# One layer's experts, batch by batch, inside the next stage of a one-core kernel

## The chip, the cores and the metric

The kernel runs on one core of a Trainium2 chip. Its time is the device time of one execution in microseconds (us), as the median of several runs. The engines are TensorE (PE; its weight loads are shown as PEld), VectorE (DVE), ScalarE (ACT), GpSimd (POOL) and SyncE (SP, which issues the DMAs). Each runs its own instruction stream in order; they meet only at semaphores and at barriers between blocks and stages.

## What is computed

The input x has 2 batches of 512 tokens with 128 features. Four layers are added to it in turn:

```python
x = x + L0_xcond(layernorm(x), ...)   # stage A: self attention, cross attention, gated feed forward
x = x + L0_ffn(layernorm(x), ...)     # stage B: rms norm, causal attention, router, 31 experts and a shared one
x = x + L1_xcond(layernorm(x), ...)   # stage C: six layers of self attention, cross attention, feed forward
x = x + L1_ffn(layernorm(x), ...)     # stage D, run in the tail of stage C: a router and 64 experts
```

The part that the change is about is the end of the second and the beginning of the third:

```python
gates = jnp.sum(jax.nn.one_hot(topi, E_R) * topv[..., None], axis=-2)          # 3 of 31 experts
h = jax.nn.gelu(jnp.einsum('bsd,edh->besh', an, re_w1) + re_b1[None, :, None, :])
routed = jnp.einsum('bse,besh,ehd->bsd', gates, h, re_w2) + jnp.einsum('bse,ed->bsd', gates, re_b2)
return shared + routed + an + attn_out
```

Every expert is computed for every token and weighted with its gate, which is zero for most. The shared expert is the 32nd, with a gate of one.

## The kernel before

The 1024 tokens are T = 8 tiles of P = 128 tokens; B = 2 batches have TB = 4 tiles each. `m.x` is the residual stream, `m.y` the running sum of a layer, `m.xn` a normalised copy, and `m.hT` its transpose, [128 features, 2 batches, 512 tokens].

`build` (L141) runs stage A, B and C one after the other. `next_stage` (L154) clears and frees every semaphore taken since the last one and puts a barrier of all engines between stages; `m.sem` takes a semaphore and notes it for that. Two semaphores are taken ahead of stage A and used in both stages (L186): `m.later_loaded`, for the load of the affine weights of 18 later norms (`normw_later`, issued at L1067 in stage A), and `m.bias_loaded`. In stage B `norm_block` "B0n" normalises x twice (`norm_steps`: statistics of all tiles, a chain of small 128x8 operations for the reciprocal root, and one apply per tile); on PE it waits for later_loaded, runs `embed` (72 small matmuls at L222), and then transposes xn (L369). Meanwhile SP loads the attention weights (L1045) and the experts' weights in eight chunks (L1146). `self_attention_block`, another norm block and `router_b` follow.

`experts_b` (a block of its own) has 32 experts, and per expert e and batch b: an "up" matmul of 128x512 into bank b (L1246), a gelu on ACT (L1281), a "down" of four 128x128 matmuls (L1254), and four additions y = y + gate * down on DVE (L1300). PE's order is up(e, b), down(e-1, b), batches alternating. f32 matmuls appear as two records each.

Stage C begins behind a barrier. SP loads the first layer's weights (`w`), the rotary tables, the masks and `wx`, the weights of all layers' cross-attention keys and values. POOL sets constants (L2158 to L2163, L2192) and builds the selector `sel` with eight affine_selects (L2196). DVE computes the layer norm of x for all eight tiles (`norm_steps`), then unit 0's first norm (L2363 to L2375), then constants. A unit is one layer for one batch; there are 12. Their work is laid out by hand in tables of slots (TENSOR, VECTOR, SCALAR, GPSIMD, SYNC, by operation): unit n's operation in slot s stands at n * WINDOW + s with WINDOW = 1214, and each engine issues its list in the order of these numbers. A slot is no time: it gives only the order. Unit 0 begins with NORM1 at slot 364, its projections (L1844, L1851), the split of q and k into three bf16 parts by DVE, ACT and POOL, and their stacking by 12 DMAs (L2091); the first scores (L1765) stand at slot 581 and their row maxima (L2384) from 594 on. The second batch, unit 1, enters 1214 slots later, so nothing stands beside unit 0 until then. The K and V tables of cross attention (`tables`) are worked in between unit 0's first 26 scores.

`merged` sorts a second list of steps in with the units' own; so far only stage D's steps (`experts_plan`) use it. Banks of PSUM are handed out by `take` (a fixed bank) and `fill` (a ring of banks 5 to 7), with a "filled" and an "emptied" semaphore for each.

## Time and profile before

| | us |
|---|---|
| median of 3 runs | 2744.12 (2743.93 to 2749.65) |
| the profiled execution, its time | 2760.86 |
| its span, first to last instruction | 2759.1 |
| mean granted PE clock in it | 0.898 |

The profile page gives each engine's busy time over the span. A view by windows cuts the span and gives busy times, the granted clock (1.00 is 2.4 GHz, 0.50 is 1.2 GHz) and the DMA share in each window. The timeline lists instructions in order of time, with the idle time of the engine before them and what ended it.

### The profile page before, as it was taken

What the parts mean: (1) busy time and instruction counts of PE and PEld (TensorE: products, weight loads), DVE (VectorE), ACT (ScalarE), POOL (GpSimd) and SP (SyncE); (2) the same over time, 40 slices, a digit from 0 to 9 for tenths busy, and PEclk for the clock granted to TensorE, in tenths of its full rate; (3) what the DMA queues carried; (4) which work ended last, traced back from release to release, by engine and by line L of the source; (5) the groups of instructions that cost most, each with busy time, mean ns of one, the idle gap of its engine ahead of it and who ended that gap; (6) DMA issues with size and microseconds to landing.
All of it is one profiled execution on the core that took longest, in us unless ns stands there. A gap on an engine that the chain in (4) does not pass through costs nothing.

```text
span 2759.1 us, 32148 instructions
## 1 busy us (share of the span) xinstructions
PE 2273.3 (82%) x11288; PEld 900.5 (33%) x11288; DVE 1707.3 (62%) x3854; ACT 1132.3 (41%) x1855; POOL 143.3 (5%) x143
## 2 busy tenths in 40 slices
PE   5999969589999594698788788778878878877898
PEld 2333334343333373222222322223223232222433
DVE  4666748525666467676577567467657746755464
ACT  2333323102222131356366455646636645553421
POOL 0000000011110003000000000000000000010000
PEclk9999979769999697679799888979979988997999
DMA  3000000110000001000010001001001000020000
GB/s 137 1 1 1 1 0 1 65 43 1 1 1 1 1 1 65 26 24 1 23 40 1 24 1 40 1 24 40 2 23 40 1 24 1 24 96 0 1 0 8
DMA packets 38033, 54.33 MB, mean 20 GB/s; under 512 B 5074, under 2 KB 34547, under 8 KB 36339
## 3 DMA queue, kind: packets, MB, share of 16 engines
q1 hardware_dynamic: 37874, 52.28, 6.0%
q8 instruction: 93, 1.52, 0.2%
q14 instruction: 66, 0.53, 0.1%
HBM read 32.34 MB, written 0.52 MB: 12 GB/s over the span
## 4 chain that ended last, share of the span: by engine, by line
PE 38%; DVE 11%; ACT 8%; issue 4%; SPq 0%; ACTq 0%; DMA 0%; DVEq 0%
PE ps L1799 7%; PE ps L1784 5%; ACT C_prob L2226 4%; PE ps L1765 4%; DVE C_nm L2384 3%; PE ps L1844 3%; PE ps L1903 2%; PE ps L2012 2%; PE ps L1915 2%; ACT C_u L2304 2%; PE ps L2008 2%; PE ps L2033 2%; PE ps L1922 2%; PE ps L1880 2%; PE ps L1931 2%
## 5 line engine op out<-in xcount | busy, mean ns | idle before, releaser
L2384 DVE TENSOR_REDUCE C_nm<-ps 128x1 f32<-128x512 f32 x768 | 501.1, 684 | 207.7 <-PE ps L1765 202.7
L2226 ACT ACTIVATE C_prob<-ps 128x512 f32<-128x512 f32 x768 | 427.5, 596 | 248.6 <-PE ps L1784 238.8
L1765 PE MATMUL ps<-C_attn 62*128 62x512 bf16 x768 | 285.3, 428 | 65.9 <-DVE C_nm L2384 45.7
L1784 PE MATMUL ps<-C_attn 64*128 64x512 bf16 x768 | 259.6, 407 | 62.9 <-ACT C_prob L2226 52.0
L1799 PE MATMUL ps<-C_prob,C_attn 128*32 128x512 f32 x1536 | 223.4, 656 | 13.8 <-ACT C_prob L2226 13.8
L1765 PEld LDWEIGHTS ps<-C_attn 62*128 62x128 bf16 x768 | 64.6, 95 | 316.6 <-DVE C_nm L2384 153.1
L1784 PEld LDWEIGHTS ps<-C_attn 64*128 64x128 bf16 x768 | 59.5, 94 | 285.5 <-ACT C_prob L2226 204.5
L711 DVE TENSOR_REDUCE A_nm<-ps 128x2 f32<-128x1024 f32 x64 | 77.5, 1211 | 113.8 <-PE ps L494 113.7
L2304 ACT ACTIVATE C_u<-ps,C_biasx 77x512 f32<-77x512 f32 x192 | 115.5, 678 | 53.6 <-PE ps L1907 53.4
L2480 DVE TENSOR_REDUCE C_nmx<-ps 128x4 f32<-128x308 f32 x192 | 78.4, 470 | 60.7 <-PE ps L1884 60.5
L644 ACT ACTIVATE A_p<-ps 128x1024 f32<-128x1024 f32 x64 | 65.6, 1025 | 112.1 <-PE ps L522 112.1
L644 ACT ACTIVATE B_p<-ps 128x1024 f32<-128x1024 f32 (+1 forms) x64 | 45.0, 703 | 146.7 <-PE ps L526 146.7
L2639 DVE TENSOR_TENSOR C_prob<-C_prob,ps 128x512 f32<-128x512 f32 x64 | 43.9, 686 | 94.2 <-PE ps L2012 74.3
L2346 ACT ACTIVATE C_prob<-ps 128x512 f32<-128x512 f32 (+1 forms) x66 | 39.4, 597 | 151.9 <-PE ps L2008 149.6
L1844 PE MATMUL ps<-C_hT,C_w 128*128 128x512 f32 x144 | 89.1, 729 | 11.6 <-ACT C_hT L2250 6.2
L1300 DVE SCALAR_TENSOR_TENSOR y<-ps,B_gates,y 128x128 f32<-128x128 f32 x256 | 71.9, 344 | 42.0 <-PE ps L1254 42.0
L452 PE MATMUL ps<-hT,B_w 128*128 128x512 f32 x128 | 75.6, 674 | 23.4 <-DVE B_rot L706 12.2
L1880 PE MATMUL ps<-C_kc,C_qx 32*128 32x308 f32 x384 | 49.0, 584 | 41.9 <-DVE C_nmx L2480 20.0
L1838 PE MATMUL ps<-ident,xn 128*128 128x128 f32 x144 | 27.4, 321 | 67.4 <-DVE xn L2375 67.4
L494 PE MATMUL ps<-A_k,A_q 64*128 64x512 f32 x256 | 76.1, 672 | 4.9 <-DVE A_nm L711 4.9
L1254 PEld LDWEIGHTS ps<-B_w,B_h 128*128 128x128 f32 x512 | 68.1, 194 | 30.7 <-issue 30.7
L2406 DVE RECIPROCAL C_rden<-ps 128x16 f32<-128x16 f32 x96 | 24.3, 253 | 82.8 <-PE ps L1807 53.3
(376 smaller groups left out, 3855.1 us busy)
## 6 DMA issues: line engine op xcount, KB each, us to landing
C_attn<-C_first SPq DMA_DIRECT2D x144, 128.0 KB, 2.4
C_w<-in_C_w SPq DMA_DIRECT2D x6, 1090.0 KB, 5.1
C_attn<-in_D_ew SPq DMA_DIRECT2D x4, 1536.0 KB, 11.1
B_w<-in_B_ew SPq DMA_DIRECT2D x8, 514.0 KB, 10.8
normw_later<-in_norm_w SPq DMA_DIRECT2D x1, 2304.0 KB
A_w<-in_A_w SPq DMA_DIRECT2D x2, 1024.0 KB, 11.5
A_w<-in_A_w SPq DMA_DIRECT2D x2, 768.0 KB, 7.9
B_w<-in_B_w SPq DMA_DIRECT2D x1, 1536.0 KB, 9.7
```

Source lines behind the costliest of these rows:

```text
L494: last = pe.matmul(ps[:, S_BANK + h, 0:keys(t)], lhsT=qT[half(h), n % 3, t * P:(t + 1) * P], rhs=kT[half(h), n % 3, 0:keys(t)], start=True ...
L644: act.activation(prob[:, n % 2, kt, :, q0:S], ps[:, ST_BANK:ST_BANK + 2, q0:S], ACT.Exp, scale=SCALE)\
L711: dve.tensor_reduce(nm[:, n % 2, t, :], ps[:, S_BANK:S_BANK + 2, 0:keys(t)], AX.X, ALU.max, negate=True).then_inc(max_done, 1)
L1765: pe.matmul(ps[:, bank, :], lhsT=qs[side(hp, MAX_ROW), b, 2 * q + pq, t * P:(t + 1) * P], rhs=ks[side(hp, MAX_ROW), b, 2 * q + pq, :], sta ...
L1784: pe.matmul(ps[:, bank, :], lhsT=ks[side(1 - hp, HALF), b, 2 * q + pq, kt * P:(kt + 1) * P], rhs=qs[side(1 - hp, HALF), b, 2 * q + pq, :], ...
L1799: last = pe.matmul(ps[ct * VW:(ct + 1) * VW, PV_BANK, :], lhsT=va[:, b, kt, q * QUAD + ct, :], rhs=prob[:, kt % 2, ct // 2, ct % 2, :], st ...
L1844: pe.matmul(ps[:, bank, :], lhsT=weight(n, col), rhs=hT[:], start=True, stop=True)\
L1880: pe.matmul(ps[:, banks[r], 0:4 * CTX], lhsT=qx[rows, t * P:(t + 1) * P], rhs=cross.k[rows, c, :, :], start=True, stop=False)
L2226: act.activation(prob[:, kt % 2, pq, 1 - hp, :], ps[:, bank, :], ACT.Exp, scale=SCALE)\
L2304: act.activation(probx[:, q % 2, r, :], ps[0:CTX, bank, :], ACT.Exp, bias=cross.bias[:, b:b + 1], scale=SCALE).then_inc(emptied[bank], 1)
L2384: dve.tensor_reduce(nm[:, q % 2, t, pq, hp:hp + 1], ps[:, bank, :], AX.X, ALU.max, negate=True).then_inc(emptied[bank], 1)
L2480: dve.tensor_reduce(nmx[:, t, 4 * r:4 * r + 4], ps[:, bank, 0:4 * CTX].rearrange("p (j k) -> p j k", k=CTX), AX.X, ALU.max, negate=True).t ...
```

## The change

The experts of stage B leave their own block and become steps of stage C's order.

- `experts_b` is gone. The new list `first_plan` puts its work at negative and early slots: `bias_b`, then 65 steps `expert` on PE, ACT and DVE, first the 32 of batch 0 (20 slots apart, from slot -475 to 165) and then the 32 of batch 1 (18 slots apart, to 741 on PE). Step k on PE is up(k) followed by down(k-1). `up_bank` alternates banks 0 and 1 for batch 0 and is bank 2 alone for batch 1; `down_bank` alternates 3 and 4. The hidden tile h has two buffers, in place of four.
- The layer norm of x at the start of stage C is made batch by batch (`first_norm`, three parts each): batch 0 at slots 196 to 232, batch 1 at 772 to 852. DVE's constants come in ten parts among batch 0's experts.
- The cross-attention tables are steps of the plan too (`tables_v` from slot 861, `tables_k` from slot 921). `wx` is loaded only after the last expert, since its place in memory now holds the experts' weights.
- Memory is shared: the experts' weights with `prob` and `shared`, h and the transposed gates with `cw` and `cwx`, the gates and b2 with `cn`. Waits are added where the sharing asks for them (the first EXP, the first COPY_SUMS, the first WEIGH).
- The load semaphores change: later_loaded is taken inside stage A, counts both late loads, and SP waits for it at stage A's end. The waits for it and for bias_loaded in stage B are gone. The experts' chunks share one semaphore, for which SP waits in `router_b`.

```diff
-            m.later_loaded, m.bias_loaded = m.sem("later_loaded"), m.sem("B1_bias_loaded")
...
             if later is not None:
-                normw, w_loaded = later
-                pe.wait_ge(w_loaded, 16)
-                embed(pe, m, normw, 18, emb_done)
+                embed(pe, m, later, 18, emb_done)
...
-            if rope is not None:
-                act.wait_ge(bias_loaded, 16)
...
+    later_loaded = m.sem("later_loaded")
...
+        @block.sync
+        def _(sp):
+            sp.wait_ge(later_loaded, 32)
+
...
+            sp.wait_ge(experts_loaded, 16 * (E_MOE // B_CHUNK + 1))
...
+B_STRIDE = 20
+B_STRIDE_1 = 18
+FIRST_NORM = 110
+B_LAST = VECTOR[0]["STATS1"][0] - FIRST_NORM
+B_FIRST = B_LAST - 30 - E_MOE * B_STRIDE
+B_END = B_LAST + E_MOE * B_STRIDE_1
+WX_LOAD = 90
+WX_STRIDE = 30
+CONST_PARTS = 10
+PROB_FREE = 8 * S // EW
+
+
+def first_plan():
+
+    plan = {"PE": [], "ACT": [], "DVE": []}
+    plan["PE"] += [(B_FIRST - 4, "bias_b", b, 0) for b in range(B)]
+    plan["DVE"].append((B_FIRST - 4, "residual", 0, 0))
+    plan["DVE"] += [(B_FIRST + 1, "bias_b", b, 0) for b in range(B)]
+    for k in range(B * E_MOE + 1):
+        at = B_FIRST + min(k, E_MOE) * B_STRIDE + max(k - E_MOE, 0) * B_STRIDE_1
+        plan["PE"].append((at, "expert", 0, k))
+        if k < B * E_MOE:
+            plan["ACT"].append((at + 10, "expert", 0, k))
+            plan["DVE"].append((at + 30, "expert", 0, k))
+    for i in range(CONST_PARTS):
+        plan["DVE"].append((B_FIRST + (18 + i) * B_STRIDE + 31, "consts", 0, i))
+    for i in range(3):
+        plan["DVE"] += [(B_LAST + 1 + i * B_STRIDE_1, "first_norm", 0, i), (B_END + 1 + 40 * i, "first_norm", 1, i)]
+    at = B_END + WX_LOAD
+    for b in range(B):
+        plan["PE"].append((at + b * WX_STRIDE, "tables_v", b, 0))
+        plan["ACT"].append((at + b * WX_STRIDE + 12, "tables_v", b, 0))
+    for l in range(LAYERS):
+        plan["PE"].append((at + (B + l) * WX_STRIDE, "tables_k", l, 0))
+        plan["DVE"].append((at + (B + l) * WX_STRIDE + 12, "tables_k", l, 0))
+    return plan
...
+        up_bank = lambda k: k % 2 if k < E_MOE else ST_BANK
+        down_bank = lambda k: ST_BANK + 1 + k % 2
...
+                def expert(k):
+                    if k < B * E_MOE:
+                        b, e = divmod(k, E_MOE)
+                        bank = take(("up_b", k), up_bank(k))
+                        pe.matmul(ps[:, bank, :], lhsT=e_b.w[:, e, 0:P], rhs=m.hT[:, b, :], start=True, stop=True)\
+                            .then_inc(filled[bank], 1)
+                    if k:
+                        e = (k - 1) % E_MOE
+                        drained(pe, ("up_b", k - 1))
+                        bank = take(("down_b", k - 1), down_bank(k - 1))
+                        for t in range(TB):
+                            last = pe.matmul(ps[:, bank, t * P:(t + 1) * P], lhsT=e_b.h[:, (k - 1) % 2, t * P:(t + 1) * P],
+                                             rhs=e_b.w[:, e, P:2 * P], start=True, stop=True)
+                        last.then_inc(filled[bank], 1)
...
+                    if at >= B_END and not moved:
+                        moved = True
+                        arrived(sp, ("down_b", B * E_MOE - 1))
+                        arrived(sp, ("down_b", B * E_MOE - 2))
+                        sp.dma_start(wx, a["C_wx"]).then_inc(cross_loaded, 16)
...
+                def expert(k):
+                    bank = arrived(act, ("up_b", k))
+                    if k >= 2:
+                        arrived(act, ("down_b", k - 2))
+                    act.activation(e_b.h[:, k % 2, :], ps[:, bank, :], ACT.Gelu,
+                                   bias=e_b.w[:, k % E_MOE, 2 * P:2 * P + 1]).then_inc(emptied[bank], 1)
...
+                def expert(k):
+                    b, e = divmod(k, E_MOE)
+                    bank = arrived(dve, ("down_b", k))
+                    if e:
+                        drained(dve, ("down_b", k - 1))
+                    for t in range(TB):
+                        y = m.y[:, b * TB + t, :]
+                        if e and t < TB - 1:
+                            dve.wait_ge(y_added, (k - 1) * (TB - 1) + t + 1)
+                        dve.scalar_tensor_tensor(y, ps[:, bank, t * P:(t + 1) * P], e_b.gates[:, b * TB + t, e:e + 1], y,
+                                                 ALU.mult, ALU.add).then_inc(y_added if t < TB - 1 else emptied[bank], 1)
```

## Rows read from the trace of the kernel before

**Rows 1.** The page, busy time of each engine, share of span, instructions.
```profile
PE 2273.3 (82%) x11288; PEld 900.5 (33%) x11288; DVE 1707.3 (62%) x3854; ACT 1132.3 (41%) x1855; POOL 143.3 (5%) x143
```

**Rows 2.** By windows: us, busy (x instructions) PE, PEld, DVE, ACT, POOL; clock, DMA, GB/s.
```profile
947.40:960.30 12.90, 12.86 (x33) 8.06 (x34) 3.73 (x7) 3.34 (x4) 0.00 (x0) 0.50 0.00 0
960.30:1071.00 110.70, 107.87 (x625) 79.00 (x623) 72.04 (x254) 41.91 (x61) 0.00 (x0) 1.00 0.00 1
1071.00:1104.40 33.40, 0.00 (x0) 0.00 (x0) 31.11 (x63) 0.00 (x0) 25.47 (x17) 0.53 0.35 135
1104.40:1135.80 31.40, 16.36 (x41) 6.25 (x41) 14.28 (x36) 6.63 (x13) 4.05 (x3) 0.69 0.21 55
1135.80:1240.80 105.00, 91.11 (x382) 25.64 (x382) 76.18 (x177) 49.21 (x89) 3.58 (x3) 0.72 0.06 16
1371.50:1472.80 101.30, 90.68 (x477) 29.33 (x469) 73.16 (x168) 60.33 (x107) 4.85 (x4) 0.89 0.10 28
```

**Rows 3.** Timeline, experts' loop: start us, us, engine, line, operation [idle <-releaser].
```profile
1060.96 1.02 PE L1246 MATMUL ps<-hT,B_w 128*128 128x512 f32 x2
1061.17 1.13 DVE L1300 SCALAR_TENSOR_TENSOR y<-ps,B_gates,y 128x128 f32<-128x128 f32 x4 [0.63 <-PE ps L1254]
...
1061.83 1.05 PE L1254 MATMUL ps<-B_w,B_h 128*128 128x128 f32 x8
...
1062.03 0.69 ACT L1281 ACTIVATE B_h<-ps,B_w 128x512 f32<-128x512 f32 x1 [1.06 <-PE ps L1246]
...
1062.72 1.02 PE L1246 MATMUL ps<-hT,B_w 128*128 128x512 f32 x2
```

**Rows 4.** Timeline at the start of stage C, VectorE and GpSimd.
```profile
1074.65 10.90 DVE L93 TENSOR_SCALAR lnv<-mv 128x8 f32<-128x8 f32 x1
...
1075.12 3.50 POOL L2163 MEMSET C_attn<- 128x4096 f32 x1
...
1086.76 12.12 POOL L2196 TENSOR_SCALAR_AFFINE_SELECT C_selx<-C_selx 128x1232 bf16<-128x1232 bf16 x8
...
1099.49 0.87 DVE L2363 BATCH_NORM_STATS2 st<-y 128x6 f32<-128x128 f32 x4
...
1103.19 1.11 DVE L2375 TENSOR_SCALAR xn<-y,mv,rs 128x128 f32<-128x128 f32 x4
```

**Rows 5.** Timeline of unit 0's projections, stacking and first scores.
```profile
1106.50 3.75 PE L1844 MATMUL ps<-C_hT,C_w 128*128 128x512 f32 x4 [0.96 <-ACT C_hT L2250]
...
1114.31 7.79 SPq L2091 DMA_DIRECT2D C_attn<-C_first  x12
...
1124.15 0.61 PE L1765 MATMUL ps<-C_attn 62*128 62x512 bf16 x2 [11.09 <-DMA C_attn<-C_first]
...
1134.39 2.48 DVE L2384 TENSOR_REDUCE C_nm<-ps 128x1 f32<-128x512 f32 x4 [1.05 <-PE ps L1765]
```

**Rows 6.** Timeline of the first norm of stage B.
```profile
538.86 1.64 DVE L115 BATCH_NORM_STATS2 st<-x 128x6 f32<-128x128 f32 x8 [1.57 <-PEq L158]
540.15 13.82 SPq L1146 DMA_DIRECT2D B_w<-in_B_ew  x8
...
543.64 2.14 DVE L127 TENSOR_SCALAR y<-x,mv,rs 128x128 f32<-128x128 f32 x8
...
550.78 2.19 DVE L125 SCALAR_TENSOR_TENSOR xn<-y,rs,rows 128x128 f32<-128x128 f32 x8
...
550.90 15.52 PE L222 MATMUL ps<-condT,normw_later 128*128 128x2 f32 x72 [15.12 <-DMA B_w<-in_B_ew]
...
566.28 1.95 PE L369 MATMUL ps<-ident,xn 128*128 128x128 f32 x8
```

**Rows 7.** Timeline of stage B's attention, a GpSimd operation and the VectorE one beside it.
```profile
805.13 1.37 POOL L443 TENSOR_TENSOR B_q<-B_rot 128x512 f32<-128x512 f32 x1 [10.18 <-DVE B_rot L706]
...
806.27 0.75 DVE L706 SCALAR_TENSOR_TENSOR B_rot<-ps,B_bias,B_cos 128x512 f32<-128x512 f32 x1 [0.89 <-PE ps L452]
```

**Rows 8.** The load of C_wx (L2127), from issue to landing.
```profile
DMA to landing us min/median/max: 8.5/8.5/8.5
```

More of the change, by code:

```diff
@@ L39 @@
 E_R = 31
+EW = 2 * P + 1
 TOPK_PAD = 40
@@ L390, in self_attention_block @@
     consts_set = sem("consts_set")
-    bias, bias_loaded = biases if biases is not None else (None, None)
     q_done, k_done, v_done = sem("q_done"), sem("k_done"), sem("v_done")
@@ L1792, in weigh @@
                     drained(pe, ("st", n, 2 * g + 1, 1))
+                    if n == 0 and g == 0:
+                        for k in range(2):
+                            drained(pe, ("down_b", B * E_MOE - 1 - k))
                     if g == 0:
@@ L2067, in last_stage @@
                         last.then_inc(filled[bank], 1)
-                for late, what in merged(TENSOR, plan["PE"]):
+                for late, what in merged(TENSOR, early_plan["PE"] + plan["PE"]):
                     if late:
-                        last_stage(*what)
+                        apart(*what)
                     else:
@@ L2346, in last_stage @@
                         act.activation(eg[0:r, k % 2, :], ps[0:r, GATE_BANK, :], ACT.Silu).then_inc(silu_done, 1)
-                for late, what in merged(SCALAR, plan["ACT"]):
+                for late, what in merged(SCALAR, early_plan["ACT"] + plan["ACT"]):
                     if late:
-                        last_stage(*what)
+                        apart(*what)
                     else:
@@ new lines, in apart @@
+                def apart(name, b, e):
+                    x = m.x[:, b % B * TB:(b % B + 1) * TB, :]
+                    if name == "residual":
+                        c_.after(dve.tensor_tensor(m.y[:], m.y[:], m.xn[:], ALU.add))
+                    elif name == "bias_b":
+                        bank = arrived(dve, ("b2", b))
+                        dve.tensor_tensor(tiles(b), tiles(b), ps[:, bank, :].rearrange("p (t d) -> p t d", t=TB), ALU.add)\
+                            .then_inc(emptied[bank], 1)
+                        drained(dve, ("b2", b))
+                    elif name == "expert":
+                        expert(e)
+                    elif name == "consts":
+                        consts(e)
+                    elif name == "first_norm":
+                        first_norm(b, e)
+                    elif name == "tables_k":
+                        tables_k(b)
+                    elif name == "norm":
@@ L2653, in last_stage @@
                             .then_inc(emptied[bank], 1)
-                for late, what in merged(VECTOR, plan["DVE"]):
+                for late, what in merged(VECTOR, early_plan["DVE"] + plan["DVE"]):
                     if late:
-                        last_stage(*what)
-                    elif what[0] or what[1] not in early:
+                        apart(*what)
+                    else:
                         step(*what)
```

316 lines of the change are left out of this document (140 added, 176 removed).

## The prediction

> **What bounds the kernel now.** I read the page first: TensorE is busy 82% of the span and no other engine comes near it [rows 1]. That is an average over stages, so the second view is busy time by window around the stages that the change touches [rows 2]. It shows four different limits one after the other. From 960.3 to 1071.0 (the experts of stage B) PE is busy 107.9 of 110.7 us at clock 1.00: the stage is bound by matmuls. From 1071.0 to 1104.4 PE does nothing at all for 33.4 us, while VectorE (31.1 busy) and GpSimd (25.5) work. From 1104.4 to 1135.8 PE is busy 16.4 of 31.4 us. Only after 1135.8 is the six-layer stage in its stride, with PE at 91.1 of 105.0 us, VectorE 76.2, at mean clock 0.72. So PE-bound work stands directly ahead of 65 us in which PE is mostly idle, in the same program, divided by a stage boundary. The third view, the timeline, says what the holes are. The first hole is one chain on VectorE, the norm of all eight tiles: a 128x8 operation took 10.90 us (L93) beside three 3.50 us memsets of GpSimd, and the chain then crawls beside eight affine_selects, until the last xn is written at 1104.3 [rows 4]. The same eight-tile norm in stage B, with GpSimd quiet, ran from 538.86 to 545.78, 6.9 us, against 1072.3 to 1099.5, 27.2 us [rows 4, 6]. The second hole is the latency of one lone batch: projections from 1106.5, the stacking DMAs from 1114.31, the first scores at 1124.15 [rows 5].
>
> There is a third, unrelated hole. At the start of stage B PE begins the 72 embedding matmuls (L222) only at 550.90, "<-DMA B_w<-in_B_ew", and ends them at 566.4; the transposes L369 stand behind them in PE's queue and start at 566.28, although xn was finished at 552.97 [rows 6]. Their own weights, normw_later, were sent for in stage A. In the code `m.later_loaded` is taken before stage A, and `next_stage()` clears and frees every semaphore taken so far; stage B's first new semaphore is `w_loaded[0]`, which counts the first experts' chunk. PE waits for a number on a semaphore that now belongs to another transfer. The row's releaser says the same.
>
> **Part 1, the freed semaphore.** The change takes later_loaded inside stage A, lets SyncE wait for it at that stage's end, and drops the waits on PE, ScalarE and VectorE in stage B. SyncE has nothing queued behind it there but the stage boundary, and both loads were issued some 530 us earlier, so the wait costs nothing. PE can then start L222 at about 538.9 and end at 538.9 + 15.5 = 554.4; xn is ready at 552.97, so the transposes start at 554.4 in place of 566.3. Next latest is PE's own embedding, so not all of 550.9 - 538.9 can be lost again. **Gain 11.9**; bounds 10 (a late start by something else) and 12.
>
> **Part 2, batch 0's experts (slots -475 to 165).** Nothing of the layers is beside them. Same matmuls, gelus and additions as now, 32 in place of 64. Steady pace from the timeline: L1246 at 1060.96, L1254 at 1061.83, next L1246 at 1062.72, so 1.75 us for one expert and batch (rounded over several such steps), with one gelu of 0.69 and four additions of 1.13 in its shadow [rows 3]. In the new order up(k) stands before down(k-1): gelu(k) has down(k-1) and up(k+1) to finish behind, 1.75 us, and needs 0.69. The additions leave VectorE 0.62 us of every 1.75. So 32 x 1.75 = 56 us, as before. The start is slow now (12.9 us at clock 0.50, in which the bias matmuls and about two and a half pairs were done: 12.9 - 2.5 x 1.75 = 8.5 extra [rows 2]) and stays so. A stage boundary in place of a block boundary: 1.3 more.
>
> In this shadow go GpSimd's constants (25.5 us), the loads of C_w and the tables, and VectorE's small constants (ten parts of under 1 us). GpSimd is the doubtful one, since it held VectorE in L93. The nearest row for an addition that reads one operand in PSUM and one in SBUF is L706: it took 0.75 us beside GpSimd's L443 from 806.27 on and lost nothing [rows 7]. I take 0, and keep 15 us as the other end (a rival below). The Trainium skill, "SBUF — State Buffer", "Who interferes with whom", has the rule: a VectorE instruction with at most one SBUF input, outside the two-port modes, does not contend with GpSimd, while tensor_scalar in such a mode blocks fully. By it L93 (tensor_scalar) waits and the additions do not; the trace agrees at both places.
>
> **Part 3, batch 1's experts (slots 165 to 741) among unit 0.** PE: 32 x 1.75 = 56; unit 0's transposes, four projections and values, some 5.6 at full clock (one projection is the size of an "up", 0.87); 11 score matmuls of 0.39, 4.4. Sum 66. From k = 32 on "up" has a single bank (bank 2), so up(k+1) waits for gelu(k): gelu starts 1.07 after its up and takes 0.69 [rows 3], 1.76, plus 0.05 to 0.15 for the release: 0.06 to 0.15 a pair, 2 to 5 us if nothing else fills it; I take 4. VectorE: 32 x 1.13 = 36; the norm of batch 0 (new `first_norm`: residual 0.7 and a 4-tile chain), 5.5 to 6, by STATS1 to APPLY1 of now, 1099.49 to 1104.30 = 4.8 [rows 4], which comes as well; seven rotations and splits of 0.69, 4.8; 12 row maxima of 0.62 to 0.69, 8. Sum 61, under PE's 66 but close, and in one queue with it: the six norm parts of 1 to 2 us each come while PE has two banks to run ahead in. I add 3. ScalarE: 22 + 5. The stacking DMAs now take from 1114.31 to 1124.15, 9.8 us, until the first score [rows 5]; in the new order 122 of the stretch's 576 slots lie between the two, some 15 us of 73; no wait. Together 66 + 4 + 3 = 73; bounds 66 and 90.
>
> **The sum to a common point.** The point is the row maximum of slot 783, the twelfth, now at 1135.8 [rows 5]. Now: 1135.8 - 947.4 = 188.4 us. After: 1.3 + 8.5 + 56 + 73 = 138.8. **Gain 49.6**; bounds 32 and 57.
>
> **Part 4, what is pushed behind that point.** `first_norm` of batch 1 (slots 772 to 852), 6 us on VectorE, and the V tables (4 matmul groups, four copies on ScalarE), which now come before it. The six K tables lie behind it in both kernels. VectorE is busy 76.2 of 105.0 us there [rows 2], so part of the 6 us fits in its gaps; PE is busy 91.1. I charge 6; bounds 9 and, if PE enters this stretch at the higher clock and keeps it (a later pair of batches, 1371.5 to 1472.8, does as much of the slots in 101.3 us with more beside it and clock 0.89 [rows 2]), a gain of 4. The C_wx load moves behind the last expert, because its place is the experts' memory. It landed 8.5 us after its issue, among other loads [rows 8]; PE wants it at slot 861, behind about ten row maxima and two norm parts, 11 us. SyncE's next duty is slot 872, so nothing stalls behind its wait. Cost 0, bound 3.
>
> **Total.** 11.9 + 49.6 - 6 = 55.5. The profiled execution took 2760.9 (span 2759.1 and 1.8 around it) and would take 2705. The median of the timed runs is 2744.1, 0.6% lower; such a difference of profile and run does not touch these stretches more than others, so 2744.1 - 55.5 = **2689**, its own range 2681 to 2697.
>
> **Rivals.** (a) The merged order stalls. In batch 1's stretch ScalarE waits in its queue for GpSimd's K splits (PART_K2), with gelus behind it, and each late gelu holds the single bank. At 0.5 us a pair, 16 us: 2705. Against it: only one gelu stands between the two splits. (b) The clock swings in batch 1's stretch as it does after 1135.8, where PE is 87% busy at mean 0.72 [rows 2]. 66 us of PE work at 0.72 take 26 more: 2715. In the Trainium skill, "TensorE: Matmul & The Clock Gate", section "A second HAM failure mode: psum-queue depth-cycling", PE working through PSUM banks with short idles between is described as swinging between the two clocks; the single bank makes such idles. Against it here: expert matmuls held 1.00 for 110.7 us [rows 2]. (c) **The other side:** the same, but at 1.2 GHz all through batch 1's stretch, +66, so that the gain is gone: 2755, slower by 0.4%. It decides once PE is at the lower level for over nine tenths of that stretch. For it: lower clock through 12.9 us of dense matmuls at 947.4. Against it: it rose then and stayed. (d) GpSimd holds the additions during its 25.5 us: 10.9 for the memsets and half of the 12 us of selects, less VectorE's slack: +15, 2704. (e) L222 still starts late, by something that moves with the experts' loads: 2701. (f) The tail gives back: VectorE's gaps swallow the norm and the clock stays up, and no stalls: gain 68, 2676.
>
> **How the numbers follow.** Forecast 0.50, (a) 0.13, (b) 0.11, (c) 0.03, (d) 0.05, (e) 0.05, (f) 0.12, no effect at all 0.01. A range of 2674 to 2711 leaves out (b), (c), the last and little tails. 0.2% (5.5 us) is about what a measurement of this kernel can tell from no change: faster 0.96, same 0.01, slower 0.03.
>
> **What would show it.** L222 at about 539 and L369 at 554. Pace of batch 0's experts 1.75 us from the first GpSimd memset on, four additions in 1.13 throughout; no hole of PE over 2 us between the first expert and the last; last "down" about 139 us after the first bias matmul; clock 1.00 until then. If the last expert is right and the end is not, the charge of part 4 was wrong.

## The result, and the profile after

The changed kernel takes **2683.97 us**, median of 4 runs (2671.86 to 2693.05), beside 2746.89 of the kernel before in the same rounds (4 runs, 2743.93 to 2750.2): ratio 0.9757 [0.9735, 0.9779]. Forecast were 2689, in a range of 2674 to 2711. Two repetitions gave 2685.5 and 2683.66. The profiled execution has a span of 2691.2 against 2759.1, so 67.9 less, where the sum had said 55.5. The sign, the size and most steps came out; the 12 us between 55.5 and 67.9 are the interesting part.

The page of the kernel after, span, busy time and, in 40 slices, the granted clock:

```profile
span 2691.2 us, 32165 instructions
PE 2259.9 (84%) x11288; PEld 897.5 (33%) x11288; DVE 1687.6 (63%) x3866; ACT 1132.4 (42%) x1855; POOL 142.9 (5%) x143
PEclk8999979859999699799798799889979989988999
```

It answers to [rows 1]: the same matmuls in a shorter span, VectorE 20 us less busy (its stalled chain is gone). Busy time by window over the stretch that the change rebuilds, with the columns of [rows 2]; the bounds are the end of the copy of the gates, the clock's rise, the first "up" of batch 1, the first row maximum, the twelfth, and unit 1's first:

```profile
937.40:947.20 9.80, 8.71 (x29) 6.40 (x30) 2.64 (x4) 2.66 (x3) 8.75 (x7) 0.52 0.69 219
947.20:999.70 52.50, 52.50 (x302) 38.16 (x302) 36.05 (x138) 20.61 (x30) 16.53 (x11) 1.00 0.07 26
999.70:1036.20 36.50, 34.87 (x182) 23.66 (x181) 30.02 (x121) 13.32 (x22) 0.00 (x0) 1.00 0.00 1
1036.20:1075.60 39.40, 34.92 (x182) 23.27 (x180) 29.30 (x92) 12.56 (x19) 3.88 (x3) 1.00 0.21 61
1075.60:1152.20 76.60, 64.94 (x251) 18.09 (x251) 58.47 (x154) 35.59 (x64) 3.57 (x3) 0.75 0.09 27
```

The 33.4 us of a PE that does nothing and the 31.4 us at half load [rows 2] are gone. In batch 0's experts PE is busy 52.50 of 52.50 us while GpSimd works for 16.53; in batch 1's it is busy 69.8 of 75.9. The clock is 1.00 for 128 us, then 0.75 where it had been 0.67 before the change.

**The ledger of the 67.9 us**, by stations that both traces have (first norm of stage B, its first rotation, the router's logits, the end of the gates' copy, the twelfth row maximum, unit 1's first, the end):

| stretch | before | after | gained | forecast |
|---|---|---|---|---|
| to the start of stage B | 538.9 | 536.1 | 2.8 | 0 |
| to the first rotation | 32.9 | 20.5 | 12.4 | 11.9 |
| to the router's logits | 361.3 | 366.8 | -5.5 | 0 |
| to the end of the gates' copy | 14.0 | 14.0 | 0 | 0 |
| gates' copy to twelfth maximum | 188.5 | 138.2 | 50.3 | 49.6 |
| to unit 1's first maximum | 77.0 | 76.6 | 0.4 | -6 |
| to the end | 1546.4 | 1539.0 | 7.4 | 0 |

The two terms that the change was priced by are right within 1 us. Four rows that were priced at 0 or at -6 are not. The first of them, 2.8, is chance: in the fourteen profiles of this document stage B starts between 534.7 and 538.9, and in the two repetitions of the changed kernel at 538.8 and 536.0. The other three need the experiments.

### The profile page after: what moved, and what is told of

It is laid out like the page before. It is cut to its first block, busy times and chain, and to the rows that moved or that the text cites. A ratio compares the mean times of both kernels' runs of the same rounds, so it can differ in the third digit from the quotient of the medians.

```text
span 2691.2 us, 32165 instructions
## 1 busy us (share of the span) xinstructions
PE 2259.9 (84%) x11288; PEld 897.5 (33%) x11288; DVE 1687.6 (63%) x3866; ACT 1132.4 (42%) x1855; POOL 142.9 (5%) x143
## 4 chain that ended last, share of the span: by engine, by line
PE 38%; DVE 10%; ACT 7%; issue 4%; SPq 0%; DMA 0%; ACTq 0%; DVEq 0%
PE ps L1762 7%; PE ps L1744 5%; ACT big L2220 4%; PE ps L1725 4%; DVE C_nm L2392 4%; PE ps L1807 2%; PE ps L1886 2%; PE ps L1993 2%; PE ps L1898 2%; PE ps L1989 2%; PE ps L2014 2%; PE ps L1905 2%; PE ps L1863 2%; ACT big L2300 2%; PE ps L1914 2%
## 5 line engine op out<-in xcount | busy, mean ns | idle before, releaser
L2220 ACT ACTIVATE big<-ps 128x512 f32<-128x512 f32 x768 | 427.8, 596 | 235.6 <-PE ps L1744 226.3
L1725 PE MATMUL ps<-C_attn 62*128 62x512 bf16 x768 | 277.6, 418 | 57.9 <-DVE C_nm L2392 47.0
L1744 PE MATMUL ps<-C_attn 64*128 64x512 bf16 x768 | 253.4, 398 | 62.3 <-ACT big L2220 51.7
L1762 PE MATMUL ps<-big,C_attn 128*32 128x512 f32 x1536 | 213.8, 630 | 13.3 <-ACT big L2220 13.3
L2300 ACT ACTIVATE big<-ps,C_biasx 77x512 f32<-77x512 f32 x192 | 115.5, 678 | 55.9 <-PE ps L1890 55.8
L2354 ACT ACTIVATE big<-ps 128x512 f32<-128x512 f32 (+1 forms) x66 | 39.4, 597 | 149.0 <-PE ps L1989 146.7
L2695 DVE TENSOR_TENSOR big<-big,ps 128x512 f32<-128x512 f32 x64 | 44.0, 687 | 92.1 <-PE ps L1993 73.8
L2605 DVE SCALAR_TENSOR_TENSOR y<-ps,cn,y 128x128 f32<-128x128 f32 x256 | 72.0, 344 | 34.6 <-PE ps L1836 33.7
L1836 PEld LDWEIGHTS ps<-big,pair 128*128 128x128 f32 x512 | 67.5, 193 | 33.6 <-issue 30.8
L2327 ACT ACTIVATE pair<-ps,big 128x512 f32<-128x512 f32 x64 | 44.0, 687 | 78.1 <-PE ps L1829 78.0
## 6 DMA issues: line engine op xcount, KB each, us to landing
C_attn<-in_D_ew SPq DMA_DIRECT2D x4, 1536.0 KB, 10.2
```

The lines of the kernel that those rows point to most:

```text
L1725: pe.matmul(ps[:, bank, :], lhsT=qs[side(hp, MAX_ROW), b, 2 * q + pq, t * P:(t + 1) * P], rhs=ks[side(hp, MAX_ROW), b, 2 * q + pq, :], sta ...
L1744: pe.matmul(ps[:, bank, :], lhsT=ks[side(1 - hp, HALF), b, 2 * q + pq, kt * P:(kt + 1) * P], rhs=qs[side(1 - hp, HALF), b, 2 * q + pq, :], ...
L1762: last = pe.matmul(ps[ct * VW:(ct + 1) * VW, PV_BANK, :], lhsT=va[:, b, kt, q * QUAD + ct, :], rhs=prob[:, kt % 2, ct // 2, ct % 2, :], st ...
L2220: act.activation(prob[:, kt % 2, pq, 1 - hp, :], ps[:, bank, :], ACT.Exp, scale=SCALE)\
L2300: act.activation(probx[:, q % 2, r, :], ps[0:CTX, bank, :], ACT.Exp, bias=cross.bias[:, b:b + 1], scale=SCALE).then_inc(emptied[bank], 1)
```

## Experiments

"Kernel before" and "changed kernel" are what an edit starts from. Each time is the median of its runs, the ratio is to the kernel before in the same rounds.

**1. Part 1 alone.** The kernel before, where only the two semaphores of stage A's late loads are no longer among those that the stage boundary frees:

```diff
-m.later_loaded, m.bias_loaded = m.sem("later_loaded"), m.sem("B1_bias_loaded")
+m.later_loaded, m.bias_loaded = (nc.alloc_semaphore(name=n) for n in ("later_loaded", "B1_bias_loaded"))
```

> The kernel before with the two late loads' semaphores taken where no stage clears them; nothing else. Theory (part 1 stands alone): L222 starts with stage B and not 12 us later, the first projections of stage B come 12 us earlier, and the time falls by 12 us, ratio 0.9955. Rival (given back): the attention that follows starts 12 us nearer to PE's idle time and runs longer at the lower clock, as in the first profile of the changed kernel, where 5.5 of 12.4 us were lost again before the router: 7 us, ratio 0.9975. Rival (the wait was a real one, for something else): 0.

Measured: 2735.93 (12 runs), ratio 0.9935 [0.9912, 0.9958], beside 2752.14: 16.2 us less, by the interval 12 to 24, so the forecast 12 lies at its edge and the 7 of the rival outside it. Its timeline on PE at the start of stage B, and the same in the changed kernel (start, length, idle before and who ended it):

```profile
536.30 14.47 PE L222 MATMUL ps<-condT,normw_later 128*128 128x2 f32 x72 [3.08 <-PEq L158]
550.64 1.95 PE L369 MATMUL ps<-ident,xn 128*128 128x128 f32 x8
```
```profile
536.11 14.50 PE L231 MATMUL ps<-condT,normw_later 128*128 128x2 f32 x72 [3.09 <-PEq L159]
...
548.04 2.19 DVE L126 SCALAR_TENSOR_TENSOR xn<-y,rs,rows 128x128 f32<-128x128 f32 x8
...
550.47 1.95 PE L376 MATMUL ps<-ident,xn 128*128 128x128 f32 x8
```

The embedding begins with the stage; the idle of 15.12 us that a DMA of B_ew ended [rows 6] has become 3.08 that the stage boundary ends. From stage B's start to its first rotation it is 20.9 against 32.9. Of these 12.0 the way to the router's logits gives 5.8 back (367.1 against 361.3), as in the changed kernel. No work is added there; it is the clock. Two windows over stage B's attention, and in the fence behind them the one of the kernel before that begins, like the second, 23 us after the first rotation:

```profile
554.40:580.00 25.60, 19.15 (x42) 6.84 (x42) 6.69 (x10) 0.60 (x1) 3.69 (x7) 0.50 0.15 47
580.00:620.00 40.00, 33.84 (x136) 13.52 (x136) 14.08 (x21) 7.51 (x10) 5.88 (x5) 0.76 0.00 1
```
```profile
595.00:635.00 40.00, 34.23 (x158) 13.63 (x158) 15.42 (x23) 8.32 (x11) 6.43 (x5) 0.91 0.00 1
```

136 matmul records in the 40 us against 158, at a mean clock of 0.76 against 0.91. Between the embedding and the logits the clock was at its lower level for 76.6 us here and 59.5 in the kernel before.

**2. All but Part 1.** The changed kernel, with a wait for the first expert chunk put back ahead of the embedding:

```diff
+                pe.wait_ge(m.first_chunk, 16)
                 embed(pe, m, later, 18, emb_done)
...
-            sp.dma_start(e.w[:, part, :], a["B_ew"][part].rearrange("e p c -> p e c")).then_inc(w_loaded, 16)
+            sp.dma_start(e.w[:, part, :], a["B_ew"][part].rearrange("e p c -> p e c"))\
+                .then_inc(w_loaded if i else m.first_chunk, 16)
```

> The changed kernel with PE made to wait, ahead of the embedding matmuls, for the landing of the first chunk of experts' weights, as it did by accident before; all else as changed. Theory: 7 to 12 us slower than the changed kernel, so 2691 to 2696 if that is 2684. Rival (the wait is hidden elsewhere): no difference from the changed kernel.

Measured: 2696.88 (6 runs), ratio 0.9795 [0.9761, 0.9828], so 11.4 above the changed kernel in the same rounds (2685.5), where 7 to 12 were expected. (The router's wait for the experts' chunks counts one less in this kernel.) PE's row has the old cause again:

```profile
548.36 15.52 PE L231 MATMUL ps<-condT,normw_later 128*128 128x2 f32 x72 [14.61 <-DMA big<-in_B_ew]
```

First rotation 32.4 after the stage's start, logits 361.3 after that: both as before the change, and the lower clock again for 59.5 us. The wait is the cause of the 12 us, from both sides. Over twelve profiles (all but 11 and 12, in which the router's loads were moved) the way to the logits is a line of 0.31 us for each us at the lower clock, with no point more than 0.9 off it. The lower clock had 59.5, 65.9 and 59.5 us in the three kernels that wait, and 52.1 to 76.6, mean 68.2, in the eleven that don't: some 2 us given back on average. Eleven profiles and three whose ranges overlap don't show that the earlier start is its cause; that stays open.

**3. The interleave taken away, the merged stage kept.** The changed kernel with unit 0's first norm put behind the last expert:

```diff
-FIRST_NORM = 110
+FIRST_NORM = 710
-WX_LOAD = 90
+WX_LOAD = 690
```

> Batch 1's experts are put ahead of all of unit 0 (FIRST_NORM 710 in place of 110), the tables stay at their slots. GpSimd's constants and the loads are still hidden by experts, but the projections, splits, stacking and first scores of unit 0 stand alone again. Theory (both holes are filled by experts, and the second is worth as much as the first): from the last expert to the twelfth row maximum some 40 us in place of 5, less about 12 us of PE work that leaves the stretch: 22 to 28 us slower than the changed kernel, 2706 to 2712. Rival (the gain is the hidden constants and norm alone, and the interleaving only moves work): under 8 us slower, 2684 to 2692.

Measured: 2708.69 (6 runs), ratio 0.9831 [0.9798, 0.9864], 23.2 above the changed kernel. Windows of this kernel, the third from batch 1's first "up" to the twelfth maximum, and PE in its timeline behind the last expert:

```profile
943.80:996.80 53.00, 53.00 (x304) 38.42 (x303) 36.35 (x140) 20.63 (x30) 16.40 (x11) 1.00 0.07 26
996.80:1097.80 101.00, 75.50 (x360) 48.24 (x358) 63.95 (x229) 26.32 (x41) 4.06 (x3) 0.86 0.09 28
```
```profile
1071.55 1.11 PE L1801 MATMUL ps<-ident,xn 128*128 128x128 f32 x4 [11.83 <-DVE xn L2383]
1073.58 3.51 PE L1807 MATMUL ps<-C_hT,C_w 128*128 128x512 f32 x4 [0.91 <-issue]
```

From the gates' copy to the twelfth maximum: 188.5 before, 163.9 here, 138.4 in the changed kernel. So the stretch's 50 us split into 24.6 for the constants, loads, GpSimd's work and batch 0's layer norm that now lie under experts, and 25.5 for the order in which batch 1's experts stand in the latency of unit 0's start. The second part is the 11.83 us in front of the transposes and the lone projections and stacking of [rows 5]. It isn't pure interleaving: the edit also puts batch 1's layer norm, which the changed kernel makes after the last expert, ahead of unit 0's own norm. VectorE in this kernel, first and last row of batch 1's layer norm, then the last of unit 0's:

```profile
1061.09 0.69 DVE L2613 TENSOR_TENSOR x<-x,y 128x512 f32<-128x512 f32 x1
...
1065.52 1.11 DVE L2625 TENSOR_SCALAR y<-x,mv,rs 128x128 f32<-128x128 f32 x4
...
1070.38 1.11 DVE L2383 TENSOR_SCALAR xn<-y,mv,rs 128x128 f32<-128x128 f32 x4
```

5.5 of the 11.83 us are that layer norm. A kernel with the experts apart and the norm later was not run; by subtraction, an estimate from these rows, the interleaving alone is worth about 20.

**4. and 5. The price of a single bank.** First one bank for all "up"s, then two for all but the last nine:

```diff
-        up_bank = lambda k: k % 2 if k < E_MOE else ST_BANK
+        up_bank = lambda k: 0 if k < E_MOE else ST_BANK
```

> The changed kernel with one bank for the up matmuls of batch 0 too (bank 0), in the stretch where nothing else is beside the experts. It measures the price of the single bank by itself. By the prediction's sum (gelu 1.07 after its up, 0.69 long, 0.05 to 0.15 for the release) the pace of batch 0 goes from 1.75 to between 1.81 and 1.91, 2 to 5 us over 32 experts; the trace of batch 1 says 1.90, so 4.8 us. Rival (in batch 1 it is something else that makes 1.90, such as VectorE's lag): batch 0 stays at 1.75.

```diff
-        up_bank = lambda k: k % 2 if k < E_MOE else ST_BANK
+        up_bank = lambda k: k % 2 if k < 55 else ST_BANK
```

> The changed kernel with two banks for the up matmuls (0 and 1, by turns) as far as the first scores allow, to expert step 54; from 55 on bank 2 alone. Theory: of batch 1's steps some 13 stand with no other PE work between them, and each gets 0.15 back, 2 us from the first up of batch 1 to the twelfth row maximum (76 us now); where projections or norm parts stand between, nothing. Rival (the stretch is bound by VectorE's queue): 0. A timed difference to the changed kernel of 2 us is below what these runs can tell; the stations in the trace are to tell it.

Measured, in the same rounds: 2699.58 (ratio 0.9814 [0.9785, 0.9842]) and 2686.33 (0.9764 [0.9731, 0.9797]). PE in batch 0's experts with one bank, and in batch 1's of the changed kernel, where it also has one:

```profile
961.06 1.13 PE L1829 MATMUL ps<-hT,big 128*128 128x512 f32 x2
962.02 1.05 PE L1836 MATMUL ps<-big,pair 128*128 128x128 f32 x8
962.96 1.13 PE L1829 MATMUL ps<-hT,big 128*128 128x512 f32 x2
```
```profile
1001.49 1.13 PE L1829 MATMUL ps<-hT,big 128*128 128x512 f32 x2
...
1003.40 1.12 PE L1829 MATMUL ps<-hT,big 128*128 128x512 f32 x2
```

A pair takes 1.90 or 1.91 where two banks give 1.75, with no idle in the row: the wait shows as an "up" of 1.13 in place of 1.02, which a look for PE's holes would miss. In batch 0 the bank costs 31 x 0.15 = 4.7 and some 2 more at the half-clocked start: gates' copy to twelfth maximum 145.2 against 138.4. The other way, 23 of batch 1's "up"s with a second bank save only 1.5 from its first to its last "up" (68.1 against 69.6), where 23 x 0.15 would be 3.5: the rest was filled by unit 0's matmuls. Its time can't be told from the changed kernel's. The two times differ by 13 us, more than banks explain: the stretch has 8.0 of it (145.1 against 137.1), and the rest lies in stretches that neither edit touches.

**6. Batch 1's norm away.**

```diff
-                        for t in range(TB):
+                        for t in range(0 if b else TB):
...
+                    elif b:
+                        pass
```

> The changed kernel without batch 1's layer norm in stage C: the residual is added, but its statistics, reciprocal root and the normalised copy are left out, so unit 1 and all that follows work on other numbers. It takes 5.3 us of VectorE work out of slots 772 to 852. The step of the prediction that charged 6 us: from the twelfth row maximum to unit 1's first one, 76.6 and 72.7 us in two profiles, falls by 5 to 6. Rival (VectorE's gaps there take the norm in, as the two profiles suggest against 77.0 before): it falls by under 2.

Measured: 2679.89 (4 runs), ratio 0.9747 [0.9717, 0.9778]. What the norm does in the changed kernel, on VectorE and then on PE in its timeline:

```profile
1073.59 0.69 DVE L2613 TENSOR_TENSOR x<-x,y 128x512 f32<-128x512 f32 x1
1074.32 0.87 DVE L2615 BATCH_NORM_STATS2 st<-x 128x6 f32<-128x128 f32 x4
1075.22 0.38 DVE L2618 BATCH_NORM_AGGREGATE mv<-st 128x2 f32<-128x6 f32 x4
1075.63 2.01 DVE L2392 TENSOR_REDUCE C_nm<-ps 128x1 f32<-128x512 f32 x3
```
```profile
1076.38 1.20 PE L1725 MATMUL ps<-C_attn 62*128 62x512 bf16 x2 [3.42 <-DVE C_nm L2392]
```

Its first part stands ahead of three row maxima, and PE waits 3.42 us for one of them; without the norm that wait is 2.10 (the residual stays). From the gates' copy to unit 1's first maximum it takes 207.6 us, against 211.1, 210.3 and 210.9 in three profiles (8, 9 and 2) whose clock was at the lower level for about the same time from the twelfth maximum on (24 to 27 us). So the norm costs 2.7 to 3.6, not 6; 2.7 is against the profile whose time at the lower clock is the same (24). About 1 of it lies ahead of the twelfth maximum. From the twelfth maximum on it is 70.5 against 72.4 to 72.7, a fall of 2: near the rival (under 2), and not the 5 to 6 of the theory.

**7. GpSimd out of the norm's way, in the kernel before.** GpSimd's constants wait for the norm's last xn; the selector goes behind unit 0:

```diff
+                pool.wait_ge(xn_ready, 1)
                 pool.memset(krow[:], 1.0).then_inc(consts_set, 1)
...
+                    if n == 0 and s in GPSIMD[0]["LAST_K"]:
+                        selector()
```

> The kernel before with GpSimd held until unit 0's first norm is done, and the eight affine_selects put behind unit 0's K splits; no interleaving, and the late embedding as before. Theory (20 of the 27 us of the eight-tile norm were GpSimd's doing): that norm takes 7 us, the 10.90 us operation 0.17; GpSimd's memsets then delay PE's first transposes by some 2 us and hide beside the projections; 16 to 18 us less, ratio 0.994. Rival (the norm is slow by itself, or the memsets are then the path): under 5 us less, ratio above 0.998.

Measured: 2746.03 (10 runs), ratio 0.998 [0.9964, 0.9996]. Its timeline at the start of stage C, in order of time:

```profile
1068.41 1.64 DVE L115 BATCH_NORM_STATS2 st<-x 128x6 f32<-128x128 f32 x8 [1.37 <-PEq L158]
...
1070.77 0.17 DVE L93 TENSOR_SCALAR lnv<-mv 128x8 f32<-128x8 f32 x1
...
1073.19 2.14 DVE L127 TENSOR_SCALAR y<-x,mv,rs 128x128 f32<-128x128 f32 x8
...
1079.07 1.11 DVE L2380 TENSOR_SCALAR xn<-y,mv,rs 128x128 f32<-128x128 f32 x4
...
1086.56 3.50 POOL L2193 MEMSET C_attn<- 128x4096 f32 x1
1086.64 6.90 DVE L2531 TENSOR_SCALAR C_validc<-C_mkc 77x2 f32<-77x2 uint8 x1 [6.46 <-POOL C_attn L2164]
1086.66 1.11 PE L1838 MATMUL ps<-ident,xn 128*128 128x128 f32 x4 [22.38 <-POOL C_attn L2164]
```

L93 takes 0.17 in place of 10.90 [rows 4], and the last xn is there at 1080.2, 11.8 us after the stage's start, where it had been 32.0. So GpSimd was the cause. Yet PE now waits for GpSimd's memset, and the next tensor_scalar, of 77x2 elements, takes 6.90 beside the next two memsets. From the gates' copy to the twelfth maximum it is 178.3 against 188.5, but not all of that is the edit's. The experts and the start of stage C by windows, in the kernel before and in this one:

```profile
947.10:1072.30 125.20, 120.73 (x656) 87.06 (x656) 75.79 (x263) 45.25 (x65) 0.04 (x1) 0.95 0.00 1
1072.30:1135.60 63.30, 16.30 (x40) 6.18 (x40) 45.17 (x97) 6.63 (x13) 29.48 (x20) 0.60 0.29 98
```
```profile
948.00:1068.40 120.40, 115.93 (x656) 83.86 (x656) 75.80 (x262) 45.27 (x65) 0.00 (x0) 0.98 0.00 1
1068.40:1126.30 57.90, 20.01 (x40) 7.23 (x40) 31.60 (x97) 6.75 (x13) 29.16 (x20) 0.54 0.32 108
```

4.8 of the 10.2 us lie in the experts, which the edit doesn't touch: the clock rose 3.2 us after the gates' copy, and 13.2 in the kernel before. The stage that was edited is 5.4 us shorter, and the ratio says the same (about 5, by the interval 1 to 10). The 16 to 18 us of the theory didn't come; it was the rival's outcome, with the memsets on the path. So moving the blocking within the stage gives some 5 us.

**8. and 9. The changed kernel twice more.** Neither has an edit; the first came with experiments 1 to 3, the second with 10 to 12.

> The changed kernel once more, for a second profile. By the first, the ratio to the kernel before was 0.976 and about 7 of its 68 us lay where nothing was changed: units 4 and 5 took 225.0 us from first row maximum to first row maximum of unit 6, against 232.1 before. If that is the clock's chance, the second profile shows another pair of units short, or none; if it is an effect of the change, the same stretch is 225 again. In either case: the experts and unit 0 to the twelfth row maximum 138 us, the pace of batch 1's experts 1.90.

> The changed kernel a third time, beside the three below, for their comparison and as a test of the account of the chance part. Over nine profiles, the 11 units after unit 1's first row maximum, which no edit touches, took 1527.8 to 1546.4 us, in order of their time at the lower clock (229 to 287 us), about 0.33 us for each. Theory: this profile lies on that line, and from the gates' copy to the twelfth row maximum it is 138.2 to 138.4 again. Rival: the unchanged units vary apart from the clock.

Measured: 2685.5 (2680.02 to 2692.32, 6 runs; ratio 0.9747 [0.971, 0.9783]) and 2683.66 (2677.93 to 2698.61, 6 runs; 0.9768 [0.9739, 0.9797]). Spans of the profiles 2688.0 and 2679.0. The last part, from unit 1's first maximum to the end, by windows, in the kernel before, after, and these two:

```profile
1212.60:2759.00 1546.40, 1277.95 (x6634) 464.12 (x6632) 970.84 (x2499) 788.37 (x1362) 63.06 (x61) 0.91 0.06 19
```
```profile
1152.20:2691.00 1538.80, 1269.49 (x6633) 463.55 (x6632) 971.18 (x2498) 788.32 (x1362) 63.06 (x61) 0.92 0.06 19
```
```profile
1147.90:2688.00 1540.10, 1270.34 (x6633) 464.39 (x6632) 971.20 (x2498) 788.60 (x1361) 63.15 (x61) 0.91 0.06 19
```
```profile
1148.30:2679.00 1530.70, 1261.71 (x6635) 462.96 (x6632) 969.83 (x2498) 788.14 (x1361) 63.13 (x61) 0.92 0.06 19
```

The stretch from unit 4's first maximum to unit 6's took 232.1 us before, 225.0 after, and 233.8 and 228.9 in these two, so the 7 us there were chance. From the gates' copy to the twelfth maximum it is 138.5 and 137.8 (138.2 in the profile after).

The last part has the same instructions, the same busy time of VectorE and ScalarE within 1.4 us, and lengths from 1530.7 to 1546.4. Their order is that of the time at the lower clock in that part. It is 286.9 us before, 255.6 after, 263.3 and 243.7 in these two, 229.0 in experiment 1 (length 1527.8, the shortest) and 283.6 in experiment 10 (1544.6). The fourteen profiles of this document lie on one line, 0.336 us for each us at the lower level, none more than 3.1 off. Experiment 1, whose last part is that of the kernel before, has the least of all: the time at the lower clock there doesn't go with the kernel. What makes it differ from one profile to the next isn't shown.

**10. and 11. Towards a better version.** Batch 1's experts spread wider, so that more of unit 0 stands among them; and three small edits: two banks as in 5, batch 1's bias matmuls 96 slots later, and the router's two loads sent for with stage B's first loads:

```diff
-B_STRIDE_1 = 18
+B_STRIDE_1 = 24
```

> The changed kernel with batch 1's experts 24 slots apart in place of 18, so that they reach to slot 933 and stand beside unit 0's scores for longer. Theory (what unit 0 leaves of PE is worth filling anywhere before unit 1 comes): from the gates' copy to unit 1's first row maximum, 214.8 and 211.1 us in the two profiles of the changed kernel, 3 to 6 less, since PE is at the lower clock for 27 to 38 us of the 73 to 77 after the last expert and would be kept busy. Rival (banks 2 and 3 are shared with the transposed scores from slot 905, and VectorE is busy 58 of 77 us there already): equal or up to 4 more.

```diff
+        sp.dma_start(rw, a["B_rw"]).then_inc(r_loaded, 16)
+        sp.dma_start(rb, a["B_rb"].rearrange("(o e) -> o e", o=1).broadcast_to([P, E_R])).then_inc(r_loaded, 16)
...
-    plan["PE"] += [(B_FIRST - 4, "bias_b", b, 0) for b in range(B)]
+    plan["PE"] += [(B_FIRST - 4 + 96 * b, "bias_b", b, 0) for b in range(B)]
...
-        up_bank = lambda k: k % 2 if k < E_MOE else ST_BANK
+        up_bank = lambda k: k % 2 if k < 55 else ST_BANK
```

> The changed kernel with three small edits: two banks for the ups to step 54, batch 1's bias matmuls a few experts later, when the clock is up, and the router's two small loads sent with the experts' weights instead of inside the router's block. Theory: 3.3 us less in the router (PE now waits 4.25 us for the load), 1.5 to 2 for the banks as in the run with that edit alone, 1 for the bias: 6 us, ratio to the kernel before 0.973. Rival: each is swallowed by the chance part, and the stations alone show them.

Measured, in the rounds of 9 (2683.66): wide 2693.91 (4 runs, 0.9791 [0.9761, 0.982]), the three edits **2676.33** (4 runs, 0.9726 [0.9698, 0.9753]). With the wide stride the twelfth maximum comes 9 us earlier (129.0 after the gates' copy), but unit 1's first 5 to 9 later (219.4 against 214.8, 211.1 and 210.3), so neither the theory (3 to 6 less) nor the rival (up to 4 more) had the size. PE in its timeline:

```profile
1067.80 0.39 PE L1725 MATMUL ps<-C_attn 62*128 62x512 bf16 x1 [1.50 <-DVE C_nm L2392]
...
1078.64 2.07 PE L1829 MATMUL ps<-hT,big 128*128 128x512 f32 x2 [2.03 <-ACT big L2220]
1080.51 1.75 PE L1836 MATMUL ps<-big,pair 128*128 128x128 f32 x8
```

The last experts fall among unit 0's maxima and exponentials and wait for VectorE and ScalarE, and some run at the lower clock: an "up" pair of 2.07 in place of 1.13. From the gates' copy to unit 1's first maximum, in this kernel and in 9:

```profile
929.40:1148.80 219.40, 193.09 (x940) 112.73 (x940) 155.80 (x508) 87.47 (x140) 32.75 (x23) 0.92 0.12 36
```
```profile
938.10:1148.30 210.20, 189.69 (x940) 108.35 (x940) 156.32 (x507) 84.79 (x138) 32.77 (x23) 0.92 0.12 38
```

The mean clock is the same, 0.92. PE is idle for 26.3 us against 20.5 and busy 3.4 longer, so most of the loss is waiting and not the clock.

All three edits show in the trace. The router's first matmul of the kernel after and of this one:

```profile
923.41 3.62 PE L1187 MATMUL ps<-B_rw,hT 128*128 128x31 f32 x16 [4.25 <-DMA B_rb<-in_B_rb]
```
```profile
921.73 3.59 PE L1188 MATMUL ps<-router_w,hT 128*128 128x31 f32 x16 [0.94 <-PEq L348]
```

That is 3.3 us (3.0 by the line of experiment 2, at equal time at the lower clock), and the gates' copy to the twelfth maximum is 135.8 against 138.2: batch 1's first "up" comes 1.1 earlier, with the first "up" of all 3.0 us after the copy and not 4.7, and from there on the two banks save 1.3. Together 5.7; the medians say 7, and the two intervals overlap, so it is the fastest measured, by about as much as can be measured.

**12. Both together** (stride 24, two banks for k < 49):

> Both: the three small edits and the experts 24 slots apart (two banks to step 48). Theory: the sum of the two, 9 to 12 us less than the changed kernel. Rival: as for the wide one, no more than the three edits give.

Measured: 2680.95 (5 runs), ratio 0.9759 [0.9734, 0.9785]. Twelfth maximum at 125.0, unit 1's first at 214.4 against 208.1 with stride 18: the wide stride loses here as well. The expected 9 to 12 us below the changed kernel are 2.7, less than the three edits give alone.

## Why the prediction was right, and where it was not

**The diagnosis held.** The embedding waited for a freed semaphore's new owner (1, 2), and GpSimd held the norm (7: 0.17 against 10.90).

**Part 1**, 11.9: measured 12.4 and 12.0 in profiles, and by times 11.4 (2) and 16.2 (1). The step was right, its claim that nothing behind it changes was not quite: at the logits 2.3 to 5.8 us of it were gone in the kernels 1, 8, 9 and the kernel after, through the clock. The prediction weighed the clock in batch 1's stretch and nowhere else.

**Part 2**, 65.8 from the boundary to batch 1's first "up": measured 62.3. The pace was 1.75, and the start was the term that was too dear: 6.3 us in place of 1.3 + 8.5, since the clock rose 9.8 us after the gates' copy, where it had taken 12.9 [rows 2]. It came 8.6 to 10.2 us after the copy in the seven other profiles whose experts begin in the same way, and 13.2, 12.1 and 3.2 us after it in the three with the old order, so a single row could not price it. GpSimd cost nothing, as taken. The row for it was thin, since L706 lies beside L443 for only 0.23 of its 0.75 us [rows 7]; what shows it is the timeline of the kernel after, beside the memsets of C_attn:

```profile
944.76 6.95 POOL L2186 MEMSET C_attn<- 128x4096 f32 x2
...
947.41 1.13 DVE L2605 SCALAR_TENSOR_TENSOR y<-ps,cn,y 128x128 f32<-128x128 f32 x4 [4.37 <-PE ps L1836]
...
950.85 1.13 DVE L2605 SCALAR_TENSOR_TENSOR y<-ps,cn,y 128x128 f32<-128x128 f32 x4 [0.62 <-PE ps L1836]
```

Four additions take 1.13, as in [rows 3], and PE is at 100% through GpSimd's 16.53 us. Rival (d), 15 us, is out. It is what the Trainium skill's rule says ("SBUF — State Buffer", "Who interferes with whom"); the additions read one operand in PSUM, and the operations that stood still, L93 and L2531, are tensor_scalars with their input in SBUF.

**Part 3**, 73: measured 75.9. PE was busy 69.8 where I had 66 and 4 for the single bank, whose waits show as longer "up"s and not as idle (4, 5), and idle 6.1 where VectorE had been given 3. The idles are short, 1.08, 0.97 and 0.78 the longest before the last expert: the first behind a norm part on VectorE, the second behind a gelu (below), the third behind a row maximum; and 3.42 for batch 1's norm part, which the sum had put behind this point. No idle of over 2 us between the first expert and the last, as said. VectorE's terms add up to 59 or 60, not 61, which changes nothing. The last "down" ended 133.7 us after the first bias matmul, where the prediction had written about 139 for it; the twelfth maximum, for which the sum was made, came 137.1 after it. The errors of parts 2 and 3, -3.5 and +2.9, cancel: 138.2 for 138.8 is better luck than the steps are.

**Rivals (b) and (c)**, the clock: it stayed at 1.00 from 947.2 to 1075.6, so both are out. The single bank did not set it swinging, neither here nor with one bank throughout; the Trainium skill's depth-cycling ("TensorE: Matmul & The Clock Gate", "A second HAM failure mode: psum-queue depth-cycling") is not seen in that stretch. It fell only when the experts were over and PE had waited 3.42 us for a row maximum. Rival (e) left no row.

**Rival (a)** happened, once. ScalarE waited 1.78 us for GpSimd's split (L2163), its gelu came behind that at 1042.18, and PE's next "up" stood idle for it:

```profile
1042.90 1.13 PE L1829 MATMUL ps<-hT,big 128*128 128x512 f32 x2 [0.97 <-ACT pair L2327]
```

It cost 1 us where the rival had 16, for the reason that the prediction had set against it: one gelu stands between the two splits.

**Part 4** is the step that was mis-sized. It charged 6 for batch 1's norm and the V tables, with a gain of 4 as the other end. Measured: a gain of 0.4 in the profile after, and of 4.3 and 4.6 in 8 and 9, both just outside that end. Two things are in it. The norm costs 2.7 to 3.6 and not 6, and about 1 of that ahead of the twelfth maximum (6). And the part's length goes with its time at the lower clock. For the seven profiles of the changed order that have the same work in this part it is 64.4 us and 0.315 for each us at the lower clock, none more than 0.6 off. The three profiles with the old order, the kernel before, 1 and 7, lie 3.5, 3.4 and 3.3 below that line. So at equal clock norm and tables together cost 3.4 us here, and the rest of the difference is time at the lower clock: 50.9 us before, and 24 to 44 in the changed order. Experiment 1, with the old order of work, has 34.1, and 7 has 50.8. That the experts' clock is carried over, as (f) said, fits but isn't shown.

**The last 7.4 us** come from units that no edit touches. They go with the clock (8, 9), and not with the kernel as far as the profiles show: lengths over the eleven profiles with the changed order run from 1530.1 to 1544.6, mean 1537.3. The profile before (1546.4) happened to be at one end. Against that mean the change would show 9 us there, against experiment 1's profile -9.5; the three profiles with the old order have a mean of 1539.3, 2 above it. The sum of what the profiles show the change to do is 12 - 2 for Part 1, 50 for the stretch and 0 to 4 behind it, 60 to 64 us, or 57 with the 3.4 that Part 4 costs at equal clock; the three comparisons by times give 63, 67 and 64, each with an interval of some 6 to 10 us either way. The gain lies between the forecast's 55.5 and the 68 of (f). The forecast time was right by its main steps, and by some luck in that the errors of parts 2 and 3 cancel and none of the clock's 19 us of chance was in the sum.

## What to carry to other kernels

Work whose operands keep VectorE out of GpSimd's way (one of them in PSUM) is a cover to lay GpSimd's constants under; look for a tiny operation that took microseconds in a chain, and move the chain's blocker under matmuls instead of to another place on the path. Where a matmul-bound stage stands ahead of a latency-bound start, about half of the gain here came from the boundary and the other half, 20 to 25 us, from interleaving, but only up to the point where the next stage's own waits begin: spread further, the same experts lost 5 to 9 us. Take no semaphore across a boundary that frees it, and distrust a releaser in the trace that has nothing to do with the operands beside it.

## What the runs showed of the hardware

- A vector operation of 77x2 elements took 6.90 us beside two GpSimd memsets of 3.5, and one of 128x8 took 10.90 beside three of them and 0.17 with GpSimd quiet; four 128x128 additions that read PSUM took 1.13 with and without one.
- With an unchanged stream of instructions, this kernel's last 1540 us vary by 19 us with the granted clock, 0.336 us for each us at 1.2 GHz in place of 2.4. Single profiles can't be compared closer than that, but read at equal time at the lower clock they agree within 3.1.
- With one bank in place of two an expert's pair of matmuls took 1.90 us and not 1.75, and the profile shows no idle for it: the "up" reads 1.13 in place of 1.02.
- In three profiles with the same stream of matmuls behind the gates' copy the clock rose 13.2, 12.1 and 3.2 us after it; between the first and the last that made the experts 4.8 us shorter (7).
